# Delta stage of a two-block kernel: triangular inverses in two diagonal blocks of 16 with two products on TensorE; a sum in the finishing stage moved to TensorE

## The reference, cut to what matters

```python
# second block, attention: per batch and head (4 heads of 32), chunk by chunk
Kb, Vb = K * bt, V * bt
A = eye(C) + tril(Kb @ K.T, -1)
T = solve_triangular(A, eye(C), lower=True)      # the inverse of A
W, U = T @ Kb, T @ Vb
mid = U - W @ St                                 # St = S transposed
O = Q @ St + (Q @ K.T) * M @ mid                 # M: lower triangle of ones
S = S + mid.T @ K
...
x = x + attn(xn) + ffn(xn)                       # ffn: silu(gate) * up, each factor rounded to FP4 in blocks of 16
```

## Time and profile before

| | |
|---|---|
| median of 3 runs | 1620.83 us (1619.78 to 1622.5) |
| the profiled execution | 1622.98 us, of which the span from its first to its last instruction is 1621.2 us |
| granted TensorE clock, mean over the span | 0.916 of full speed |
| busy over the span | PE 1348.3 us (83%), DVE 1283.6 us (79%), ACT 863.6 us (53%), POOL 116.8 us (7%) |
| delta stage | first Gram product at 1045.3 us, last update at 1366.2 us |
| finishing stage | 1369 us to the end at 1621.2 us |

### The profile page before, as it was taken

One profiled execution on the slowest core, in us unless ns is written; L12 is line 12 of the kernel. 1 busy time (PEld: TensorE's weight loads), 2 busy tenths in 40 slices (PEclk: granted clock), 3 DMA queues, 4 the chain that ended last, 5 costly groups with the idle time before them and its releaser, 6 DMA issues. The chain is left out here.

```text
span 1621.2 us, 37551 instructions
## 1 busy us (share of the span) xinstructions
PE 1348.3 (83%) x13383; PEld 991.3 (61%) x13383; DVE 1283.6 (79%) x2864; ACT 863.6 (53%) x1583; POOL 116.8 (7%) x76
## 2 busy tenths in 40 slices
PE   0679998999999999999989999437777776778786
PEld 0566776777777777777757777325554544556665
DVE  6886117998989898989987888387778783899997
ACT  0565235777767776777757777211212211666664
POOL 2000000000000000000021222200000000221221
PEclk9868999999999999999998999757889889888888
DMA  8000002433434333333322555632222001011110
GB/s 235 1 0 0 5 4 81 121 120 117 118 112 123 116 115 117 117 118 117 119 73 75 147 155 149 214 118 81 82 82 81 30 30 61 27 58 58 59 48 30
DMA packets 122285, 142.44 MB, mean 88 GB/s; under 512 B 8768, under 2 KB 78752, under 8 KB 121120
## 3 DMA queue, kind: packets, MB, share of 16 engines
q1 hardware_dynamic: 118704, 134.81, 27.1%
q10 hardware_dynamic: 3440, 5.79, 1.0%
HBM read 106.49 MB, written 34.08 MB: 87 GB/s over the span
## 5 line engine op out<-in xcount | busy, mean ns | idle before, releaser
L1008 ACT ACTIVATE glu_a<-moe_a,b1s 128x512 f32<-128x512 f32 x256 | 176.5, 689 | 150.4 <-PE moe_a L910 121.9
L1013 ACT ACTIVATE b_raw<-moe_b,b1s 128x512 f32<-128x512 f32 x256 | 176.5, 689 | 0.8 <-PE moe_b L910 0.6
L1061 DVE TENSOR_TENSOR glu_a<-glu_a,gate_row 128x512 f32<-128x512 f32 x256 | 174.9, 683 | 0.0
L1053 DVE SCALAR_TENSOR_TENSOR glu_a<-glu_a,b_raw 128x512 f32<-128x512 f32 x256 | 174.8, 683 | 0.1
L908 PE MATMUL moe_a<-x_hi,w_hi 128*128 128x512 f32 x256 | 148.2, 579 | 5.4 <-DVE w_lo L1070 5.4
L1044 DVE TENSOR_SCALAR b_raw<-b_raw 128x512 f32<-128x512 f32 x256 | 108.1, 422 | 56.3 <-ACT b_raw L1013 54.2
L928 PE MATMUL moe_y<-glu_a,w2s 128*128 128x512 f32 x256 | 132.0, 596 | 2.6 <-DVE glu_a L1061 2.5
L910 PE MATMUL moe_b<-x_hi,w_lo 128*128 128x512 f32 x256 | 101.2, 395 | 0.0
L910 PE MATMUL moe_a<-x_hi,w_lo 128*128 128x512 f32 x256 | 101.0, 394 | 0.0
L909 PE MATMUL moe_b<-x_lo,w_hi 128*128 128x512 f32 x256 | 100.4, 392 | 0.0
L909 PE MATMUL moe_a<-x_lo,w_hi 128*128 128x512 f32 x256 | 100.3, 392 | 0.0
(11 more groups left out here) (266 smaller groups left out, 3080.6 us busy)
## 6 DMA issues: line engine op xcount, KB each, us to landing
gate_row<-gate_scratch SPq DMA_DIRECT2D x256, 256.0 KB, 3.2
kq_in<-kq_scratch SPq DMA_DIRECT2D x8, 1024.0 KB, 7.2
acc<-in_L_attn_inputs SPq DMA_DIRECT2D x8, 512.0 KB, 10.0
kq_scratch<-q_out SPq DMA_DIRECT2D x16, 256.0 KB, 2.9
xq_scratch<-qT SPq DMA_DIRECT2D x16, 256.0 KB, 2.0
v_scratch<-v_out SPq DMA_DIRECT2D x16, 256.0 KB, 2.3
k_scratch<-k_out SPq DMA_DIRECT2D x16, 256.0 KB, 2.8
k_rows_scratch<-k_rows SPq DMA_DIRECT2D x16, 256.0 KB, 3.2
```

The source lines that it names most:

```text
L1008: act.activation(glu_a[e % 4][:, :], ps_a[u][:, :], ACT.Gelu_apprx_sigmoid, bias=w["b1"][:, 0, e:e + 1]).then_inc(a_glu, 1)
L1013: act.activation(b_raw[u][:, :], ps_b[u][:, :], ACT.Identity, bias=w["b1"][:, 1, e:e + 1])\
L1053: dve.scalar_tensor_tensor(a, a, GLU_LIMIT, b_raw[u][:, :], ALU.min, ALU.mult)\
L1061: dve.tensor_tensor(a, a, gate_row[e % 4][:, :], ALU.mult).then_inc(weighted, 1)
```

## The change

Delta stage. The 32 x 32 matrix is seen as four blocks of 16. `eliminate` inverts the two diagonal blocks side by side in one instruction (a view with the stride from one diagonal block to the other): 15 columns instead of 31, each with a multiply and a subtract on 2 x (15 - j) x (j + 1) elements. The block below the diagonal, - D2 L21 D1 with D1 and D2 the inverted blocks, comes from two rounds of 128 fp32 matmuls on PE with 16 moving columns each. `cross(g)` multiplies the lower Gram block (`below`, copied out by ACT) with D1 (`dn`, a transpose by `turn_n` on DVE); `keep_half` on ACT copies the outcome out of PSUM; `join(g)` multiplies it with D2; `fix` on DVE subtracts it from `tt`. `cross(g + 1)` stands at PE's place 4 and `join(g + 1)` at place 5 of `scan(g)`, that is, around chunk 2; those of group 0 stand ahead of `scan(0)`. PSUM gains one bank, `ps_c`.

Finishing stage. The sum with `acc` becomes a matmul with the identity, first into `ps_f` (4 fp32 matmuls of 128 columns for a tile), and `finish` becomes a copy on ACT, behind `size_h`.

```diff
+        BL = CH // 2
+        STRIDE = BL * CH + BL
+        lower_flat = [sb(f"lower{i}", [P, 2 * STRIDE]) for i in range(2)]
+        tinv_flat = [sb(f"tinv{i}", [P, 2 * STRIDE]) for i in range(2)]
+        prod = [sb(f"solve_prod{i}", [P, 2, BL, BL]) for i in range(2)]
...
-        HALF = 11
-        SOLVE = 2 * (CH - 1)
+        def diagonal(flat):
+            return flat[:, :].rearrange("p (b x) -> p b x", b=2)[:, :, 0:BL * CH]\
+                             .rearrange("p b (r s) -> p b r s", s=CH)
+        lower_blocks, tinv_blocks = [diagonal(a) for a in lower_flat], [diagonal(a) for a in tinv_flat]
+        HALF = 8
+        SOLVE = 2 * (BL - 1)
+        LATE_AT = {0: 2, 1: 1, 2: 2, 3: 1, 4: 1}
+        TURN_N_AT, TURN_T_AT, FIX_AT = 5, 6, 12
         TAKE_AT = {1: 0, 3: 1, 5: 2, 7: 3}
-        PAIRS_AT = {9: 4, 10: 1, 11: 1, 13: 4, 14: 1}
-        LAST_AT = {k: (3, 1, 1)[k % 4 - 1] for k in range(16) if k % 4}
+        SOON_AT = {k: 1 for k in range(8, 16)}
+        CROSS_PLACE, JOIN_PLACE = 4, 5
...
+                def cross(g):
+                    pe.wait_ge(lt_copied, 2 * QUARTERS * (g + 1))
+                    pe.wait_ge(dn_ready, g + 1)
+                    if g == 0:
+                        pe.wait_ge(blanked, 3)
+                    else:
+                        pe.wait_ge(t_ready, g)
+                    for n in range(NCH):
+                        for rows in heads():
+                            mm = pe.matmul(ps_c[rows, n, :], below[g % 2][rows, n, :], dn[rows, n, :],
+                                           start=True, stop=True)
+                    mm.then_inc(crossed, 1)
+                def join(g):
+                    pe.wait_ge(dt_ready, g + 1)
+                    wait_before_product(pe, passed, half_ready, g + 1)
+                    for n in range(NCH):
+                        for rows in heads():
+                            mm = pe.matmul(ps_c[rows, n, :], half_way[rows, n, :], tt[g % 2][rows, n, BL:],
+                                           start=True, stop=True)
+                    mm.then_inc(joined, 1)
...
                         if g + 2 < GROUPS and place in GRAM_PLACES:
                             gram(g + 2, GRAM_PLACES[place])
+                        if g + 1 < GROUPS and place == CROSS_PLACE:
+                            cross(g + 1)
+                        if g + 1 < GROUPS and place == JOIN_PLACE:
+                            join(g + 1)
...
                 gram(1, range(QUARTERS))
+                cross(0)
+                join(0)
                 for g in range(GROUPS):
...
                     for quarter in quarters:
                         act.wait_ge(grammed, QUARTERS * g + quarter + 1)
+                        act.activation(below[g % 2][:, 8 * quarter:8 * quarter + 8, BL:],
+                                       ps_g[quarter % 2][:, :, 0, BL:], ACT.Copy,
+                                       scale=w["upper"][:, 1, BL - 1:BL]).then_inc(lt_copied, 1)
                         act.activation(lt[:, :, 8 * quarter:8 * quarter + 8].rearrange("p c n -> p n c"),
                                        ps_g[quarter % 2][:, :, 0, :], ACT.Copy).then_inc(lt_copied, 1)
+                def keep_half(g):
+                    act.wait_ge(crossed, g + 1)
+                    if g >= 1:
+                        act.wait_ge(joined, g)
+                    act.activation(half_way[:, :, 0:BL], ps_c[:, :, :], ACT.Copy).then_inc(half_ready, 1)
...
+                        if g + 1 < GROUPS and 2 * c == CROSS_PLACE:
+                            keep_half(g + 1)
                         for h in range(2):
...
-                    m, n = j + 1, CH - 1 - j
+                    m, n = j + 1, BL - 1 - j
                     if j > 0:
                         dve.wait_ge(solve[g % 2], SOLVE * (g // 2) + 2 * j)
-                    dve.tensor_tensor(prod[g % 2][:, m:, 0:m], lower[g % 2][:, m:, j:m].to_broadcast([P, n, m]),
-                                      tinv[g % 2][:, j:m, 0:m].to_broadcast([P, n, m]), ALU.mult)\
+                    dve.tensor_tensor(prod[g % 2][:, :, m:, 0:m],
+                                      lower_blocks[g % 2][:, :, m:, j:m].to_broadcast([P, 2, n, m]),
+                                      tinv_blocks[g % 2][:, :, j:m, 0:m].to_broadcast([P, 2, n, m]), ALU.mult)\
                        .then_inc(solve[g % 2], 1)
...
+                def turn_n(g):
+                    dve.wait_ge(solve[g % 2], SOLVE * (g // 2 + 1))
+                    if g >= 1:
+                        dve.wait_ge(crossed, g)
+                    dve.transpose(dn[:, :, :].rearrange("p n s -> p s n"),
+                                  tinv[g % 2].rearrange("p i c -> p c i")[:, 0:BL, :]).then_inc(dn_ready, 1)
                 def turn_t(g):
-                    dve.wait_ge(solve[g % 2], SOLVE * (g // 2 + 1))
                     if g >= 2:
                         dve.wait_ge(mid_done, STEPS * (g - 1))
-                    dve.transpose(tt[g % 2][:, :, :].rearrange("p n i -> p i n"), tinv[g % 2][:, :, :])\
-                       .then_inc(t_ready, 1)
+                    dve.transpose(tt[g % 2][:, :, :].rearrange("p n i -> p i n"), tinv[g % 2]).then_inc(dt_ready, 1)
+                def fix(g):
+                    dve.wait_ge(joined, g + 1)
+                    x = tt[g % 2][:, :, BL:]
+                    dve.tensor_tensor(x, x, ps_c[:, :, :], ALU.subtract).then_inc(t_ready, 1)
...
+                        if late < GROUPS:
+                            for _ in range(LATE_AT.get(k, 0)):
+                                eliminate((late, next(last)))
+                            if k == TURN_N_AT:
+                                turn_n(late)
+                            if k == TURN_T_AT:
+                                turn_t(late)
+                            if k == FIX_AT:
+                                fix(late)
                         if soon < GROUPS:
-                            for _ in range(ALONE_AT.get(k, 0)):
-                                eliminate((late, next(alone)))
...
-                            for _ in range(PAIRS_AT.get(k, 0)):
-                                eliminate((late, next(alone)), (soon, next(beside)))
-                        elif late < GROUPS:
-                            for _ in range(LAST_AT.get(k, 0)):
-                                eliminate((late, next(alone)))
-                    if late < GROUPS:
-                        turn_t(late)
+                            for _ in range(SOON_AT.get(k, 0)):
+                                eliminate((soon, next(first)))
-                for j in range(HALF):
-                    eliminate((0, QUARTERS + j), (1, j))
-                for j in range(QUARTERS + HALF, CH - 1):
-                    eliminate((0, j))
+                for j in range(BL - 1 - QUARTERS):
+                    eliminate((0, QUARTERS + j), *[(1, j)] * (j < HALF))
+                turn_n(0)
                 turn_t(0)
+                fix(0)
...
-                        pe.matmul(ps_f[:, j, :], oN[u][:, P * j:P * j + P], w["wo"][:, :], start=True, stop=False)
+                        pe.matmul(ps_f[:, j, :], w["ident"][:, :],
+                                  acc[:, bass.ds(SUBS * t + j, 1), :].rearrange("p a d -> p (a d)"),
+                                  start=True, stop=False)
+                        pe.matmul(ps_f[:, j, :], oN[u][:, P * j:P * j + P], w["wo"][:, :], start=False, stop=False)
...
+                def finish(t, u):
+                    act.wait_ge(down, t + 1)
+                    wait_sent(act, stored, t, u, 16)
+                    act.activation(result[u][:, :, :], ps_f[:, :, :], ACT.Copy).then_inc(final, 1)
...
-                                   (1, size_h), (0, lambda t, u: silu(t, u, (2, 3)))])
+                                   (1, size_h), (2, finish), (0, lambda t, u: silu(t, u, (2, 3)))])
...
-                def finish(t, u):
-                    dve.wait_ge(down, t + 1)
-                    wait_sent(dve, stored, t, u, 16)
-                    dve.tensor_tensor(result[u][:, :, :], acc[:, bass.ds(SUBS * t, SUBS), :], ps_f[:, :, :],
-                                      ALU.add).then_inc(final, 1)
```

More of the change, by code:

```diff
@@ L1476, in delta_pass @@
         lt = sb("lt", [P, CH, NCH])
-        lower = [sb(f"lower{i}", [P, CH, CH]) for i in range(2)]
-        tinv = [sb(f"tinv{i}", [P, CH, CH]) for i in range(2)]
-        prod = [sb(f"solve_prod{i}", [P, CH, CH]) for i in range(2)]
+        BL = CH // 2
[3 more added lines that the diff above has]
+        prod = [sb(f"solve_prod{i}", [P, 2, BL, BL]) for i in range(2)]
+        below = [sb(f"below{i}", [P, NCH, CH]) for i in range(2)]
+        dn = sb("dn", [P, NCH, BL])
+        half_way = sb("half_way", [P, NCH, CH])
         tt = [sb(f"tt{i}", [P, NCH, CH]) for i in range(2)]
@@ L1499, in delta_pass @@
         s_added, st_ready, o_copied, o_stored = sem("s_added"), sem("st_ready"), sem("o_copied"), [sem(f"o_stored{i}") for i in range(2)]
```

(22 more changed lines are left out.)

15 lines of the change are left out of this document (11 added, 4 removed).

## The result

The changed kernel takes 1711.19 us (median of 4 runs, 1708.9 to 1715.08) against 1621.66 us for the kernel before in the same session: a ratio of 1.0556, 95% interval 1.0532 to 1.058. It is slower, as forecast; the forecast of 1698 us was 13 us too low, inside its range of 1650 to 1725. The profiled execution's span went from 1621.2 to 1708.0 us, +86.8.

What follows compares the result with a forecast made beforehand. PE's code loading, one load for 126 passes in 3.77 us, was taken to bound dense code. 1622.98 us plus 84.6 for the delta stage less 8 for the finish gave 1699.6, forecast as a median of 1698, range 1650 to 1725.

Steps and rivals of the forecast that it cites:

- ahead of the recurrence: Before the first group: DVE's columns, then the two products of group 0 in series; +2 us, between -3 and +5.
- groups 0 to 5: Delta stage: each group goes from 37.3 to 49.0 us, +70.2 us for six.
- chunks 0 and 1: Delta stage, a group's first two chunks: 654 passes have a floor of 19.6 us; taken as 20.8, from 21.6.
- chunk 2: Delta stage, the chunk with both products: 711 passes, 5.64 loads, 21.3 us; taken as 21.5.
- chunk 3: Delta stage, a group's last chunk: its 5.75 us, plus `fix` and a column ahead of the second residue; 6.7 us.
- finish: Finishing stage: DVE loses the sum, 0.5 us a tile, and some waits, PE gains matmuls; -8 us, between -11 and 0.
- DVE's saving: Delta stage: with 15 columns for 31, DVE needs some 9 us less a group and no longer bounds it.
- Rival 4: Finishing stage gives nothing, its PE loop needing code loads each pass: 0 instead of -8, 1706 us; within the forecast's 0.68.
- Rival 1: Delta stage: code loading is hidden in dense code, a product costs 3.2 us; about 1632 us, chance 0.06.
- the partly overlapped load: Delta stage: a code load takes 2.8 us instead of 3.77, a group 43.5; 1659 us, chance 0.10 (1645 to 1680).
- Rival 2: Delta stage: PE's new work fits its idle time and groups shorten as DVE's work shrinks; about 1552 us, chance 0.06.
- Rival 3: Delta stage: loads run later behind waits of PE's queue, 4.3 us each in chunk 2; 1720 us, chance 0.10.

Runs made afterwards that it cites:

- e2_small: Kernel before plus 128 fp32 32x32 by 32x16 matmuls that nothing waits for at each of PE's places 4 and 5, groups 0 to 6: 1712.7 us.
- e7_half_fp32: Kernel before plus 64 unread fp32 32x32 by 32x16 matmuls (128 passes) at each of places 4 and 5, groups 0 to 6: 1658.77 us.
- e8_bf16: Kernel before plus 128 unread bf16 32x32 by 32x16 matmuls (128 passes) at each of places 4 and 5, groups 0 to 6: 1658.95 us.
- e12_loop: Kernel before plus 128 unread fp32 matmuls at each of places 4 and 5, run as a PE loop of 8 rounds over 16: 1671.05 us.
- e5_less_traffic: Changed kernel with the loads of groups 4 to 7 cut to 64 of 1024 columns: 1697.55 us.
- e4_no_products: Changed kernel with both rounds of products cut to 4 matmuls each for groups 1 to 7: 1611.9 us.
- e1_finish_only: Kernel before with the finishing stage's edit alone, delta stage as before: 1612.98 us.
- e3_wide: Kernel before plus 11 idle 512-column bf16 matmuls at each of places 4 and 5, groups 0 to 6, about the PE time of 256 small passes: 1630.71 us.

## Why the prediction was right, and where its sizes were off

**The mechanism holds.** PE in the delta stage is paced by the loading of its code, one packet of q8 for 126 passes. The forecast of 12 or 13 packets a group and 33 more in all came out as 13 in group 3 and 33 in all; the stops stand inside L1619 and L1629, with 128 and 127 passes from one to the next. That it is the code is shown by the distance of 1.2 to 1.6 us from a packet's end to each resumption, by e2_small (no dependencies, 89 of the 96 us), by e7_half_fp32 and e8_bf16 (passes count, not matmuls) and by e12_loop (an eighth of the added code, little over half the cost). The Trainium skill, "Runtime: NRT & Kernel Launch", section "Instruction fetch mechanics", has the crossing of a block mostly hidden. This trace does not agree where PE's instructions are short: five crossings in chunk 2 of group 3 show 1.2 to 2.8 us of idle PE each.

**The sum, term by term.**

| | forecast | measured |
|---|---|---|
| ahead of the recurrence | +2 | +3.25 |
| groups 0 to 5 | +70.2 | +82.5 |
| of one group: chunks 0 and 1 | 20.8 | 23.2 |
| chunk 2 | 21.5 | 19.75 |
| chunk 3 | 6.7 | 8.06 |
| group 6 | +12.4 | +11.6 |
| group 7 | 0 | +0.9 |
| finish | -8 | -11.5 |
| span | +76.6 | +86.8 |

(Forecast's sum against the profiled execution; the groups are between starts of residues, the chunks means over groups 0 to 5; group 7 and the finish meet at the end of the last update of the state, 1365.81 us before and 1464.06 after.)

The groups cost 12.3 us more than forecast, and 3.5 us of that are hidden in the total by a finish that gave more; that part is luck.

**The term that failed is chunks 0 and 1.** The step "654 passes have a floor of 19.6, I take 20.8" left 1.2 us for waits and looked at nothing but the pace of loads with quiet DMA queues. What it left out is the traffic at the groups' start, beside which code loads start late: with it cut (e5_less_traffic) chunks 0 and 1 take 21.5 us and a group 48.65, 2.4 less than in the changed kernel and close to the 49.0 forecast. A part of the 2.4 us may have come by the granted clock, which rose with it. The sign was in the kernel before, too: its chunk 0 took 10.8 us in the mean of groups 1 to 4 and 9.4 in groups 0 and 5. I had taken the mean over all. That mean was misread too: the prediction takes group 3's chunks 2 and 3 from the mean of six groups and gets 21.6 us for chunks 0 and 1, where the trace has 21.1. Its last step is half a microsecond off as well: 1699.6 less 2.15 comes to 1697.4, not 1698.

**Chunks 2 and 3** were off in opposite ways, together 27.8 us against 28.2. I gave chunk 2 5.64 loads, for the 711 passes that it runs. But in the timeline above five loads, from the resumption at 1271.44 to that at 1290.92 us, 3.9 us each, fill the chunk (1271.17 to 1292.05). The count of passes holds over a group; a chunk gets a part of a load more or less by where the boundaries fall, and the rest came in chunk 3.

**DVE's saving** was seen rightly as worthless: busy time fell by 8.3 us in group 5, forecast "some 9". e4_no_products goes beyond the forecast: even with next to no products on PE the time is that of the finishing edit alone, within 1 us.

**The finish.** The 0.5 us for a tile was right. In the regular tiles the second `add_h` started 1.37 us behind the first and starts 0.82 or 0.90 us behind it now, in turn, and their distance went from 14.15 to 13.66 us, 0.49 less. The 0.68 us of the sum do not all come back: in the timeline above the second `h_over` ends at 1595.80 + 0.88 = 1596.68 us and the second `add_h` starts at 1596.72. The term was too small by the longer tiles of the kernel before: they held 3.9 us over the regular distance, 2.5 of it waits for `fin_f` ahead of the sum. I had seen those waits in the earlier trace rows and put 2 us on them, and took that back for PE's new matmuls, which show in no distance between tiles. The 11.5 us hold scatter besides: in e1_finish_only the stretch from the last update to the end is 8.8 us shorter than in the kernel before. Rival 4 is out by e1_finish_only.

**The rivals.** Rival 1 (1632) is out by e2_small against e3_wide; the partly overlapped load (2.8 us) as well, since loads came 3.9 us apart in the median of groups 0 to 5, and none below 3.2. Rival 2 needed under 3.0. Rival 3 (1720) had the right kind of delay in the wrong chunk: it put late loads into chunk 2, where they ran at their best pace; they were late around the groups' start.
